# Attention block after a group norm on one core: the normalised input as keys, its PE transpose as values and residual

## The reference, cut to what matters

```python
xn = group_norm(x, gamma, beta)          # x: 8 images, 32 x 32 pixels, 64 channels; 8 groups
xf = xn.reshape(8, 1024, 64)
q = xf @ wq + bq;  k = xf @ wk + bk;  v = xf @ wv + bv
attn = softmax(einsum('bnc,bmc->bnm', q, k) * 64 ** -0.5, axis=-1)
out = einsum('bnm,bmc->bnc', attn, v) @ wp + bp
return (xf + out).reshape(x.shape)
```

## Time and profile before

| what | value |
|---|---|
| median of 3 runs | 201.03 us (199.39 to 201.31) |
| profiled execution: span from first to last instruction | 199.6 us |
| time of that execution besides its span | not listed by the page |
| PE busy, mean granted clock | 95% of the span, 0.965 |
| POOL, DVE, ACT busy | 72%, 68%, 56% |

### The profile page before, as it was taken

One profiled execution on the slowest core, in us unless ns is written; L12 is line 12 of the kernel. 1 busy time (PEld: TensorE's weight loads), 2 busy tenths in 40 slices (PEclk: granted clock), 3 DMA queues, 4 the chain that ended last, 5 costly groups with the idle time before them and its releaser, 6 DMA issues.

```text
span 199.6 us, 3301 instructions
## 1 busy us (share of the span) xinstructions
PE 189.2 (95%) x1226; PEld 97.3 (49%) x1226; DVE 136.1 (68%) x179; ACT 111.2 (56%) x181; POOL 143.4 (72%) x92
## 2 busy tenths in 40 slices
PE   7895989989999999999999999999999999999993
PEld 7721435533564365536454466436452646444432
DVE  3239656697569786678767685868667856909763
ACT  2519267646865466546863676546544665338611
POOL 4108559599999979999699969996999869970000
PEclk9758599999999999999999999999999999999999
DMA  5594000000000001000100010000100010001002
GB/s 169 197 393 162 0 0 3 0 0 7 0 2 0 3 13 43 3 0 2 56 0 0 2 56 2 0 0 22 36 0 2 5 53 0 0 5 53 0 9 100
DMA packets 4415, 6.95 MB, mean 35 GB/s; under 512 B 832, under 2 KB 1456, under 8 KB 4400
## 3 DMA queue, kind: packets, MB, share of 16 engines
q1 hardware_dynamic: 4400, 6.75, 9.6%
HBM read 4.59 MB, written 2.10 MB: 34 GB/s over the span
## 4 chain that ended last, share of the span: by engine, by line
PE 80%; DVE 5%; DMA 4%; issue 3%; POOL 3%; ACT 2%; SPq 1%; DVEq 0%; POOLq 0%; ACTq 0%
PE attn L846 25%; PE scores L788 24%; PE wide L759 10%; PE scores L752 4%; PE misc L870 3%; PE scores L746 3%; DVE chunk_max L582 3%; POOL prob_sum L309 2%; DMA packed<-in_packed_dram 2%; PE misc L854 2%; PE attn L746 2%; DMA max_rows<-max_T 2%; PE misc L734 1%; ACT probs L411 1%; PE misc L861 1%
## 5 line engine op out<-in xcount | busy, mean ns | idle before, releaser
L309 POOL TENSOR_TENSOR prob_sum<-prob_sum,probs 128x1024 f32<-128x1024 f32 x42 | 102.0, 2428 | 5.7
L582 DVE TENSOR_REDUCE chunk_max<-wide 128x1 f32<-128x1024 f32 x60 | 73.4, 1223 | 31.5 <-PE wide L759 31.0
L411 ACT ACTIVATE probs<-scores 128x1024 f32<-128x1024 f32 x64 | 63.1, 1022 | 29.3 <-PE scores L788 28.5
L846 PE MATMUL attn<-probs,values 128*64 128x512 f32 x256 | 62.0, 605 | 0.0
L759 PE MATMUL wide<-k_hi,q_hi 64*128 64x512 f32 x120 | 31.0, 483 | 1.8 <-DVE chunk_max L582 1.8
L846 PEld LDWEIGHTS attn<-probs,values 128*64 128x64 f32 x256 | 15.6, 136 | 26.5 <-issue 24.1
L309 POOL TENSOR_TENSOR prob_sum<-probs 128x1024 f32<-128x1024 f32 x7 | 16.7, 2380 | 11.8 <-ACT probs L411 11.8
L759 PEld LDWEIGHTS wide<-k_hi,q_hi 64*128 64x128 f32 x120 | 12.5, 185 | 22.9 <-DVE chunk_max L582 13.2
L788 PE MATMUL scores<-q_hi,step_hi 64*128 64x512 f32 x96 | 20.7, 425 | 0.5
L788 PE MATMUL scores<-q_lo,step_hi 64*128 64x512 f32 x96 | 19.2, 391 | 0.0
L788 PE MATMUL scores<-q_hi,step_lo 64*128 64x512 f32 x96 | 19.1, 391 | 0.0
(11 more groups left out here) (132 smaller groups left out, 236.7 us busy)
## 6 DMA issues: line engine op xcount, KB each, us to landing
x_T<-in_x_turned_dram SPq DMA_DIRECT2D x8, 256.0 KB, 6.4
values<-in_x_dram SPq DMA_DIRECT2D x8, 256.0 KB, 6.5
out_dram<-y_out SPq DMA_DIRECT2D x7, 256.0 KB, 2.0
out_dram<-y_out SPq DMA_DIRECT2D x2, 128.0 KB, 1.7
max_rows<-max_T SPq DMA_DIRECT2D x14, 4.0 KB
packed<-in_packed_dram SPq DMA_DIRECT2D x1, 192.0 KB, 4.5
packed<-in_packed_dram SPq DMA_DIRECT2D x1, 130.5 KB, 2.9
bp_all<-in_bp_dram SPq DMA_DIRECT2D x1, 32.0 KB, 4.1
```

The costliest lines, as they stand in the source:

```text
L309: nc.gpsimd.tensor_tensor(prob_sum[b % 2][:, :], so_far[:, :], probs[i][:, :], ALU.add).then_inc(sum_done, 1)
L411: nc.scalar.activation(probs[i][:, :], scores[flip_of(b, i)][:, :], ACT.Exp, scale=SCALE).then_inc(exp_done, 1)
L582: nc.vector.reduce_max(chunk_max[:, p, j:j + 1], made_in[:, :], AX.X).then_inc(max_done, 1)
L846: product = nc.tensor.matmul(attn[x_half * C:(x_half + 1) * C, :], values[b][:, t * C:(t + 1) * C], probs[i][:, x_half * HALF:(x_half + 1) ...
```

## The change

Queries are projected by one matrix, the product of wq and the turned wk (`w_qk`), so that the normalised input itself serves as keys. A bias of the keys adds the same to all scores of a query, which the softmax takes out; `key_shift` is kept as such a shift. `project_k` and `copy_keys` go. `turn_values` turns the normalised input on PE, four blocks of 128x128 per image; ACT copies them to `values` (`copy_values`), and DVE adds the output bias to them for the residual (`add_bias`, from PSUM; POOL does that for the first image). With that `rows_of`, `centre`, `scale`, `scale_w_vp` and the second load of x go. `normalise` moves from DVE to ACT, as two instructions. High and low parts of the keys are made of all 512 columns at once (`round_keys`, `split_keys`), and `key_steps` on DVE now reads two SBUF operands and stands between two max reductions. `group_variance` is one product in place of two. The seven sums of an image stay on POOL; in the first image `rstd_of(2)` now follows the third sum in place of the second.

The diff, cut to its core:

```diff
             load_turned(0)
             sp.dma_start(packed[:, 0:CONSTS], packed_in[:, 0:CONSTS]).then_inc(consts_loaded, DMA)
+            sp.dma_start(packed[:, CONSTS:], packed_in[:, CONSTS:]).then_inc(weights_loaded, DMA)
             load_turned(1)
-            sp.dma_start(packed[:, CONSTS:], packed_in[:, CONSTS:]).then_inc(weights_loaded, DMA)
...
-            load_x(0)
-            load_turned(2)
-            load_x(1)
-            for z in range(3, BATCH):
+            for z in range(2, BATCH):
                 load_turned(z)
-                load_x(z - 1)
-            load_x(LAST)
...
+            def split_keys(s):
+                pool.wait_ge(key_hi_done, s + 1)
                 if s >= RING:
                     pool.wait_ge(scores_made, T * (s - RING + 1))
+                nc.gpsimd.tensor_tensor(key_lo[s % RING][:, :], keyed[s % 2][:, KEYS],
+                                        key_hi[s % RING][:, :].bitcast(fp32), ALU.subtract).then_inc(key_lo_done, 1)
...
                 for i in range(1, T):
                     sum_probs(b, i)
-                    if b == 0 and i == 1:
-                        split_step(1)
-                    if b == 0 and i == 2:
+                    if b == 0 and i == 3:
                         rstd_of(2)
                 if exists(z):
                     rstd_of(z)
                 if exists(s):
-                    split_first(s)
-                    split_step(s)
+                    split_keys(s)
...
+            def normalise(s):
...
+                nc.scalar.activation(minus_mean_gain[:, s:s + 1], minus_mean[:, s:s + 1], ACT.Identity,
+                                     scale=gain_col[:, s:s + 1]).then_inc(minus_mean_gain_done, 1)
+                act.wait_ge(minus_mean_gain_done, s)
+                nc.scalar.activation(keyed[s % 2][:, 0:HALF], x_T[s][:, :], ACT.Identity, bias=minus_mean_gain[:, s:s + 1],
+                                     scale=gain_col[:, s:s + 1]).then_inc(xn_done, 1)
...
+            def copy_values(s, made_in):
+                act.wait_ge(turned_made, s + 1)
+                nc.scalar.copy(values[s][:, :], made_in).then_inc(values_done, 1)
...
                 if b > 0:
                     copy_den(b - 1, misc)
+                    if exists(s):
+                        normalise(s)
                 exp_tile(b, 4)
...
                 exp_tile(b, 5)
-                if 0 < b < LAST:
-                    scale_w_vp(b - 1)
+                if exists(s):
+                    round_k(s)
+                    shift_first_key(s)
+                if b == 0:
+                    copy_values(1, misc[:, :])
                 exp_tile(b, 6)
                 exp_tile(b, 7)
                 if exists(s):
+                    round_keys(s)
                     round_q(s, 0, scores[1][:, 0:HALF])
-                    copy_keys(s, scores[0][:, 0:HALF])
                     round_q(s, 1, scores[1][:, HALF:PIXELS])
-                    round_k(s)
-                    round_step(s)
+                    copy_values(s, scores[0][:, 0:HALF])
...
             def key_steps(s):
-                dve.wait_ge(keys_done, s + 1)
-                dve.wait_ge(step_lo_done, s - 1)
-                nc.vector.scalar_tensor_tensor(step[s % 2][:, :], scores[0][:, P:HALF], bias_k[:, 0:1],
-                                               keys[s % 2][:, 0:HALF - P], ALU.add,
-                                               ALU.subtract).then_inc(step_done, 1)
+                dve.wait_ge(xn_done, s)
+                nc.vector.tensor_tensor(keyed[s % 2][:, STEPS], keyed[s % 2][:, 0:HALF - P], keyed[s % 2][:, P:HALF],
+                                        ALU.subtract).then_inc(step_done, 1)
...
                 if b > 0:
                     invert(b - 1, misc)
-                centre(p)
-                if b == 1:
-                    scale(0)
+                    if exists(s):
+                        key_steps(s)
                 reduce_chunk(p, 5, wide)
-                if b == 1:
-                    add_bias(0)
-                scale(p)
+                if b == 0:
+                    key_steps(s)
                 reduce_chunk(p, 6, wide)
...
                     split_q(s, 0, scores[1][:, 0:HALF])
-                    key_steps(s)
                     split_q(s, 1, scores[1][:, HALF:PIXELS])
+                    add_bias(s, scores[0][:, 0:HALF])
...
+            def turn_values(s, to):
+                for tt in range(PAIRS):
+                    block = slice(tt * P, (tt + 1) * P)
+                    turned = nc.tensor.transpose(to[:, block], keyed[s % 2][:, block], identity)
+                turned.then_inc(turned_made, 1)
...
                 if i == 0 and exists(p):
-                    pe.wait_ge(keys_done, p + 1)
-                    pe.wait_ge(step_done, p - 1)
+                    pe.wait_ge(residual_done, p)
...
                 if exists(s):
-                    pe.wait_ge(xn_done, s - 1)
+                    pe.wait_ge(xn_done, s)
                     pe.wait_ge(exp_done, T * b + T)
                     project_q(s, (scores[1][:, 0:HALF], scores[1][:, HALF:PIXELS]))
-                    project_k(s, scores[0][:, 0:HALF])
+                    turn_values(s, scores[0])
```

More of the change, by code:

```diff
@@ L12, in attention_block @@
     AX = mybir.AxisListType
-    BATCH, HEIGHT, WIDTH, C = x.shape
+    BATCH, HEIGHT, WIDTH, C = out.shape
     PIXELS = HEIGHT * WIDTH
@@ L57, in attention_block @@
         w_vp = sb("w_vp", [P, P])
-        w_vp_s = [sb(f"w_vp_s{u}", [P, P]) for u in range(2)]
+        w_qk = sb("w_qk", [P, P])
         ones = sb("ones", [P, P])
@@ L84, in attention_block @@
         unused = [sb(f"unused{u}", [P, HALF]) for u in range(2)]
-        centred_T = sb("centred_T", [P, HALF])
-        xn = [sb(f"xn{u}", [P, HALF]) for u in range(2)]
+        keyed = [sb(f"keyed{u}", [P, 2 * HALF]) for u in range(2)]
         q_first = sb("q_first", [P, PIXELS])
@@ L113, in attention_block @@
         xT_loaded = [sem(f"xT_loaded{z}") for z in range(BATCH)]
-        x_loaded = [sem(f"x_loaded{z}") for z in range(BATCH)]
         max_placed = [sem(f"max_placed{u}") for u in range(2)]
@@ L330, in _ @@
                                         chunk_max[:, 0, j:j + 1].to_broadcast([P, P]), ALU.mult).then_inc(diag_done, 1)
-            split_step(0)
             first_steps(1)
-            split_first(1)
+            pool.wait_ge(values_done, 1)
+            pool.wait_ge(bias_out_done, 1)
+            nc.gpsimd.tensor_tensor(pixels(residual[0][:, :]), pixels(values[0][:, :]), per_channel(bias_out[:, :]),
+                                    ALU.add).then_inc(first_residual_done, 1)
+            split_keys(1)
             for b in range(LAST):
@@ L384, in round_q @@
                                      bias=bias_q[:, 0:1]).then_inc(q_hi_done, 1)
-            def copy_keys(s, made_in):
-                act.wait_ge(k_made, s + 1)
-                if s == 0:
-                    act.wait_ge(k_first_hi_done, 1)
-                if s >= 2:
-                    act.wait_ge(first_lo_done, s - 1)
-                nc.scalar.activation(keys[s % 2][:, :], made_in, ACT.Identity,
-                                     bias=bias_k[:, 0:1]).then_inc(keys_done, 1)
-            def round_k(s):
-                act.wait_ge(keys_done, s + 1)
-                nc.scalar.copy(k_hi[s % RING][:, :], keys[s % 2][:, :]).then_inc(k_hi_done, 1)
@@ new lines, in round_k, with shift_first_key @@
+            def round_k(s):
+                act.wait_ge(xn_done, s)
+                if s >= 2:
+                    act.wait_ge(chunk_made, T * (s - 1))
+                nc.scalar.activation(k_hi[s % 2][:, :], keyed[s % 2][:, 0:HALF], ACT.Identity,
+                                     bias=key_shift[:, 0:1]).then_inc(k_hi_done, 1)
+            def shift_first_key(s):
+                if s == 0:
+                    act.wait_ge(first_xn_done, 1)
+                    act.wait_ge(key_shift_done, 1)
+                else:
+                    act.wait_ge(xn_done, s)
+                nc.scalar.activation(keyed[s % 2][:, FIRST_KEY], keyed[s % 2][:, HALF - P:HALF], ACT.Identity,
+                                     bias=key_shift[:, 0:1]).then_inc(first_key_done, 1)
@@ L751, in project_q @@
                     rows = slice(x_half * C, (x_half + 1) * C)
-                    product = nc.tensor.matmul(to[x_half], wq2[rows, :], xn[s % 2][rows, :], start=True, stop=True)
+                    product = nc.tensor.matmul(to[x_half], w_qk[rows, :], keyed[s % 2][rows, 0:HALF], start=True, stop=True)
                 product.then_inc(q_made, 1)
+            def turn_values(s, to):
[3 more added lines that the diff above has]
+                turned.then_inc(turned_made, 1)
             def max_chunk(p, j, to):
@@ L758, in max_chunk @@
                     rows, half = slice(r * C, (r + 1) * C), slice(r * HALF, (r + 1) * HALF)
-                    product = nc.tensor.matmul(to[:, half], q_hi[p % RING][rows, chunk], k_hi[p % RING][rows, :],
```

(1 more changed line is left out.)

345 lines of the change are left out of this document (138 added, 207 removed).

## The result

The changed kernel takes **191.73 us** (median of 4 runs, 191.25 to 192.72); the kernel before, run beside it, 200.49 us (4 runs, 199.39 to 201.31). The ratio is 0.962, with a 95% interval of 0.954 to 0.971: faster. The forecast was 193.8 in a range of 190.5 to 198.5. In a later series of runs the same changed kernel took 191.36 us (6 runs, 190.65 to 192.54). The ratios leave out a run that lies over 1.5% above the fastest of its kernel in the same series; the medians are of all runs.

What follows compares the result with a forecast made beforehand. PE's own work was taken to bound the loop, with clock and reductions mattering ahead of it. Gains of 4.8 us in the loop and 2.4 ahead sum to 7.2: 201.0 - 7.2 = 193.8 us, range 190.5 to 198.5.

Steps and rivals of the forecast that it cites:

- PE bounds the loop: In the loop PE's own work is the time; 0.77 us less per image, which should last about 20.8.
- The loop as a whole: Loop's total gain: 3.85 in images two to six, 0.5 in the first, 0.5 in the seventh, about 4.8 us.
- The steps between POOL's sums: `key_steps` on DVE, ready about 103.6, goes ahead of POOL's fourth sum (near 103.87), costing PE nothing, 0.25 us to spare.
- rival 2: Loop: `key_steps` ready 0.3 us later waits for POOL's fourth sum; chunks 1.9 late per image, 200 to 205; chance 0.12.
- What `rows_of` was worth: Loop, ahead of the values' product: without its products PE gets there at 102.55 in place of 103.04, 0.5 us less.
- the term of 2.4: Ahead of the loop: first chunk 1.3 us earlier, first hole gone, output bias adding 0.2; together 2.4, ends 1.0 and 4.5.
- The first hole: First image's reductions: DVE's 1.26 us wait for PE goes with the second image's key products.
- the second hole: First image's reductions: DVE's 1.35 us wait for PE, from the second image's query product, stays.
- as nearly even, a start at 9.9: Ahead of the first query product: removed and new work taken as nearly even, so it starts at 9.9.
- Rival 3: Ahead of the loop: nothing won, `w_qk` copy delays the second image's mean, clock stays 1.2 GHz; 196.2; chance 0.14.
- rival 4: Loop: POOL becomes the bound, sums stretched by `key_steps`; images shrink by 0.3 only, 197 us; chance 0.04.
- rival 5: Loop: PE's freed time not freed, by slow turns or late exponentials; loop unchanged, 198.6 to 201 us; chance 0.04.

Runs made afterwards that it cites:

- e3: Changed kernel with two products the size of the old key products put back behind the query product, results unread: 197.97 us.
- e4: Changed kernel with three unused 64-column products put ahead of the fifth max chunk, in the last image behind it: 199.63 us.
- e1: Changed kernel with an idle DVE reduction of 512 columns put ahead of `key_steps`: 199.27 us.
- the repeat: The changed kernel run again unaltered, in a later series: 191.36 us.
- e5: Changed kernel without the two `keep_warm` calls (four and two idle products) ahead of the query product: 193.2 us.
- e10: Changed kernel with three unused 64-column products put behind the fifth max chunk where a chunk follows: 196.09 us.

## Why the prediction was right, and where its sizes were off

*PE bounds the loop.* Right: images of 20.8 as forecast, PE busy in all of it, and e3 shows that a microsecond on PE is a microsecond of time. The terms of an image: from the start of the query product to that of the next values' product it is 2.33 - 1.97 = 0.36 less by PE's timelines (109.37 to 111.70, 101.97 to 103.94), where 1.01 - 0.74 = 0.27 was forecast. The four turns take 0.59 by the chain of waits, not 0.74; a row of two turns with their start and end was too dear a model for four in a row:

```profile
102.13 0.86 PE scores L700 x2
102.98 0.59 PE scores L706 x4
103.69 0.31 PE misc L728 x2
```

From the fifth tile's start to the values' product it is 0.47 less (2.75 and 2.28), where 0.5 was forecast (its sum 101.72 + 0.43 + 0.37 gives 102.52, not 102.55, which changes nothing). The sum, 0.83, is what the third to sixth images got shorter by. The loop as a whole gave 5.7, not 4.8: the difference is 0.2 in these four images, by the turns, 0.3 in the first two together, and 0.3 in the seventh and the end.

*The steps between POOL's sums.* Right, and the part on which most hung. The prediction put `key_steps` 7.25 us behind the image's first sum (103.6 - 96.35) and the fourth sum at 7.52; it starts at 7.22, ahead of the fourth sum at 7.57, and passes; at 7.69 (e4) and 7.77 (e1) it is late, unless POOL happens to pause. So rival 2 was a true risk with its edge 0.35 us away, where the forecast left 0.25. Its price was near too: 1.65 per image where 1.9 was forecast, 199.27 in e1 where the rival's lower end was 200. By the Trainium skill's page "SBUF — State Buffer", section "Who interferes with whom", a DVE instruction with two SBUF inputs and a GpSimd instruction that reads SBUF block one another by issue order; the traces agree (0.62 or 2.60 us).

*What `rows_of` was worth.* The 0.5 was right for PE's time, but the prediction did not see that its removal also gave `key_steps` its place: with these products still ahead of the fifth chunk the steps come after the fourth sum's start, as e4 shows.

*Ahead of the loop.* Here the size failed: the term of 2.4 measured 3.2 to 4.5, which lies within the ends it was given, 1.0 and 4.5. DVE's first reduction before and after, and the last one after:

```profile
15.32 1.23 DVE L582 TENSOR_REDUCE chunk_max<-scores 128x1 f32<-128x1024 f32 x1 [0.50 <-PE scores L759]
```

```profile
11.19 1.22 DVE L547 TENSOR_REDUCE chunk_max<-scores 128x1 f32<-128x1024 f32 x1 [0.28 <-PE scores L713]
...
21.37 1.22 DVE L547 TENSOR_REDUCE chunk_max<-wide 128x1 f32<-128x1024 f32 x1 [2.04 <-PE wide L713]
```

The first reduction comes 4.13 earlier, where 1.3 was forecast. The first hole (1.26) went, as forecast; the output bias adds 0.13 (0.2 forecast); and the second hole, which was to stay, grew from 1.35 to 2.04, with the clock listed at 0.50 from 16 to 22. In the repeat the first reduction comes 2.56 earlier (12.76), and the second hole is 1.77.

So the step that was mis-sized is the one that takes the added and removed products ahead of the first query product "as nearly even, a start at 9.9", and then prices it and the turns at 1.2 GHz. The product starts at 8.88 in one profile and 9.13 in the other, 0.8 to 1.0 earlier, whatever the clock did. Where the clock stayed at 2.4 GHz, it and the turns took 1.56 (8.88 to 10.44) in place of 3.6; where it was at 1.2 GHz, as assumed, 2.88 (9.13 to 12.01), as the turns are cheaper there too (0.87, 1.5 forecast). e5 has its first exponential at 26.02 and 193.2 us, against "near 26.0" and 193.8 forecast, but that is partly luck: its first reduction comes 1.85 earlier (13.47), not 1.3, and its second hole, 2.04, takes most of the difference back.

*Rival 3* said that nothing would be won there, and 3.2 to 4.5 were. Through the first image's turns the clock stood at 2.4 GHz in the first run (9.94 to 10.60, and until past 15), and at 1.2 GHz in the repeat, where it rose near 12.0 as they ended. No run has other products in their place, so whether turns hold the clock back stays open.

*POOL.* It waits 1.07 us for the fourth image's first sum, as forecast: rival 4 is out. So is rival 5.

*The distance of median to span* was taken as 1.4; a run lies 1.85 over its own span. Of the 2.1 us between forecast and median, by the profiles, 0.9 come from the loop and 0.8 to 2.1 from ahead of it, less what this distance gives back.

## What to carry to other kernels

A VectorE instruction with two SBUF inputs beside a stream of GpSimd instructions is a question of phase: measure where it starts from the mark that the stream is tied to, and how far the next GpSimd instruction is; a half microsecond of removed or added work on a third engine can decide it. When an experiment puts back one part of a change, look whether it also shifts such a place, and place it a second time where it can't. In a start-up stretch at a changing clock, price the products at both levels and let the range say so.

## What the runs showed that was not expected

- The same program had its clock fall between 8 and 9 us in one run and not before 15 in another, with PE busy 1.00 and 0.98 of each microsecond ahead of it in both; the difference of 1.3 us in the first exponential goes through to the end (165.5 us from there in both).
- POOL paused 0.47 to 0.48 us ahead of the third image's third sum, in the changed kernel as in e1, e4 and e10; in e1 and e4 that let `key_steps` pass in an image where it would have been blocked (20.76 us in place of 22.42, and 21.23 in place of 22.41). Why POOL pauses there is not shown.
- A profile can list the granted clock at 1.00 where the products' lengths are those of 0.50 (e5, 9 to 12 us): read the column together with the length of a known product.
- Four fp32 turns of 128x128 behind dense products take 0.59 us by the chain of waits, 0.49 from their start to the next product's.
